# A new order of work in the prologue of a gated cross-attention and expert layer on one core

## The reference, cut to what matters

```python
x = x + tanh(g_xattn[0]) * xattn(layernorm(x), ctx, w_sim, b_sim, W_qv, b_qv)
x = x + tanh(g_ffn[0]) * ffn(layernorm(x), w_router, b_router, w1, b1, w2, b2)

def xattn(e, c, w_sim, b_sim, W_qv, b_qv):        # e: 4096 x 512, c: 3202 x 512
    w1, w2, w3 = w_sim[:d], w_sim[d:2*d], w_sim[2*d:]
    Sim = (e @ w1)[:, None] + (c @ w2)[None, :] + (e * w3) @ c.T + b_sim[0]
    hq_hat = softmax(Sim, axis=1) @ c
    hc_bar = softmax(max(Sim, axis=1)) @ e
    feats = concat([e, hq_hat, e * hq_hat, e * hc_bar])
    return feats @ W_qv + b_qv
```

## Time and the profile before

| | |
|---|---|
| time, median of 3 runs | 2228.9 us (2227.05 to 2230.01) |
| the profiled execution | 2228.91 us, span 2227.2 us |
| mean granted TensorE clock | 0.995 |
| PE busy | 2174.8 us |
| DVE busy | 1306.1 us |
| ACT busy | 1148.6 us |
| first block of scores on PE | from 30.93 us |
| first block of the steady loop on PE | from 71.66 us |

### The profile page before, as it was taken

One profiled execution on the slowest core, in us unless ns is written; L12 is line 12 of the kernel. 1 busy time (PEld: TensorE's weight loads), 2 busy tenths in 40 slices (PEclk: granted clock), 3 DMA queues, 4 the chain that ended last, 5 costly groups with the idle time before them and its releaser, 6 DMA issues.

```text
span 2227.2 us, 34525 instructions
## 1 busy us (share of the span) xinstructions
PE 2174.8 (98%) x12099; PEld 1129.0 (51%) x12099; DVE 1306.1 (59%) x2734; ACT 1148.6 (52%) x1747; POOL 144.8 (7%) x142
## 2 busy tenths in 40 slices
PE   5999999999999999999999997999999999999997
PEld 2444444444444444444454454656556565647464
DVE  7755566555556655554667785664656464646450
ACT  6755565565556556555533443535445363526260
POOL 0000000000000000000022222010101010010101
PEclk9999999999999999999999999999999999999999
DMA  9534444444444444344887863433333334343411
GB/s 250 132 80 106 107 113 99 112 98 91 106 108 110 98 115 98 84 103 112 246 238 207 210 174 91 145 102 104 99 107 95 108 94 112 91 118 119 128 41 24
DMA packets 485232, 266.06 MB, mean 119 GB/s; under 512 B 424388, under 2 KB 424772, under 8 KB 481084
## 3 DMA queue, kind: packets, MB, share of 16 engines
q1 hardware_dynamic: 474156, 244.90, 41.9%
q0 software_dynamic: 11024, 20.52, 4.7%
HBM read 97.96 MB, written 71.52 MB: 76 GB/s over the span
## 4 chain that ended last, share of the span: by engine, by line
PE 94%; DMA 2%; DVE 2%; SPq 1%; ACT 1%; issue 1%; POOL 0%; ACTq 0%; DVEq 0%; POOLq 0%
PE ps L1239 23%; PE ps L1255 22%; PE ps L2057 18%; PE ps L2072 18%; PE ps L1734 10%; DMA arena<-arena 1%; PE ps L369 1%; PE ps L1742 1%; DMA arena<-in_ctx 1%; PE ps L2084 0%; DVE arena L764 0%; PE ps L1755 0%; DMA arena<-in_L_ffn_w 0%; SPq L251 0%; PE ps L1251 0%
## 5 line engine op out<-in xcount | busy, mean ns | idle before, releaser
L1239 PE MATMUL ps<-arena 128*128 128x512 f16 (+1 forms) x2688 | 557.6, 358 | 4.4 <-DMA arena<-arena 2.7
L1255 PE MATMUL ps<-arena 128*128 128x512 f16 x2400 | 553.2, 379 | 0.4 <-DMA arena<-arena 0.4
L2057 PE MATMUL ps<-arena 128*128 128x320 f16 x3072 | 419.3, 299 | 3.3 <-DMA arena<-rows 3.1
L2072 PE MATMUL ps<-arena 128*128 128x512 f16 x1872 | 405.4, 379 | 0.0
L1239 PEld LDWEIGHTS ps<-arena 128*128 128x128 f16 x2688 | 250.3, 98 | 285.6 <-issue 5.7
L1255 PEld LDWEIGHTS ps<-arena 128*128 128x128 f16 x2400 | 233.5, 98 | 276.3 <-DMA arena<-arena 0.8
L1062 ACT ACTIVATE arena<-ps,arena 128x512 f32<-128x512 f32 (+1 forms) x224 | 163.5, 731 | 389.6 <-PE ps L1239 389.6
L2057 PEld LDWEIGHTS ps<-arena 128*128 128x128 f16 x3072 | 300.1, 98 | 122.7 <-DMA arena<-rows 4.7
L2072 PEld LDWEIGHTS ps<-arena 128*128 128x128 f16 x1872 | 183.1, 98 | 219.7
L780 DVE TENSOR_REDUCE arena<-arena 128x1 f32<-128x512 f32 (+1 forms) x224 | 139.8, 625 | 192.3 <-ACT arena L1062 191.6
L793 DVE SCALAR_TENSOR_TENSOR arena<-arena 128x512 f16<-128x512 f32 x192 | 144.1, 751 | 184.6 <-ACT arena L1083 184.6
(11 more groups left out here) (253 smaller groups left out, 1422.1 us busy)
## 6 DMA issues: line engine op xcount, KB each, us to landing
arena<-in_L_ffn_w SPq DMA_DIRECT2D x64, 1024.0 KB, 9.0
feats<-arena SPq DMA_DIRECT2D x48, 512.0 KB, 2.8
arena<-in_x SPq DMA_DIRECT2D x32, 512.0 KB, 3.4
rows<-arena SPq DMA_DIRECT2D x13, 774.0 KB, 3.8
out<-arena SPq DMA_DIRECT2D x16, 512.0 KB, 3.0
arena<-in_ctx SPq DMA_DIRECT2D x6, 1024.0 KB, 13.5
arena<-arena SPq DMA_TRANSPOSE x276, 3.1
arena<-in_L_xattn_W_qv SPq DMA_DIRECT2D x4, 1024.0 KB, 5.8
```

The source lines that it names most:

```text
L1239: mm = pe.matmul(out, qT[:, q, s * KD + k, :], ctxT[:, r * KD + k, a:z], start=(k == 0 and s + r == 0), stop=(k == KD - 1 and s == 1))
L1255: mm = pe.matmul(psO[q], turned, ctxN[:, j, r, :], start=(j + s + r == 0), stop=False)
L2057: mm = pe.matmul(psH[:, f % 2, h, :], w1s[:, s, k * F + f * P:k * F + (f + 1) * P], XT[:, r, k, h * HALF:(h + 1) * HALF], start=(k + s + r ...
L2072: mm = pe.matmul(psO[:, t % 2, :], hT[:, f, s, t * P:(t + 1) * P], w2s[:, r, f * D:(f + 1) * D], start=(f + s + r == 0), stop=(f == KF - 1 ...
```

## The change

The order of the prologue's work changes on all engines but GpSimd. SP issues the seven loads of the context one after the other, and the loads of the second pair of x, of `w1b` and of `bs` after them. Tiles 0 to 5 instead of 0 to 3 are turned on PE (`PET` = 6); of the two more, one is copied out by DVE and one by ACT. The two query units are turned into PSUM banks 3 and 2, ahead of the first scores. PE makes the first scores of both units in turn by chunk. ACT and DVE follow with their lists: among them `norm_hi(0)` and `norm_lo(0)` come early, `squares` comes earlier against `split_high`, `norm_weight(0)` and `tail_low` come before the last five maxima of unit 0, and ACT makes the first four probabilities of unit 0 before it moves out the blocks of unit 1's last three chunks.

```diff
@@ -400,7 +400,9 @@
     LAST = NC - 1
     XR = 4
     BLANKS = 3
-    FIRST = ((0, 1, 2, 3, 5, 7, 8), (4, 6, 9, 10, 11, 12, 13))
+    FIRST = ((1, 2, 4, 5, 8, 9, 10), (0, 3, 6, 7, 11, 12, 13))
+    MAXES0 = 9
+    PET = 6
     assert TILES[LAST][1] - TILES[LAST][0] == 2 and JT == 2 * NPAIR
 
     take, off = cutter(arena)
@@ -451,7 +453,7 @@
     psN = [ps[:, 4 + n, 0:NC] for n in range(2)]
     psV = ps[:, 7, 0:P]
     psT = [ps[:, 6 + n, :].bitcast(F16).rearrange("p (k i) -> p k i", i=P) for n in range(2)]
-    psQ = ps[:, 3, :].bitcast(F16).rearrange("p (k i) -> p k i", i=P)
+    psQ = [ps[:, 3 - n, :].bitcast(F16).rearrange("p (k i) -> p k i", i=P) for n in range(2)]
     psY_first = ps[:, 2:4, :]
     psX, psH = ps[:, 0, 0:P], ps[:, 1, 0:KD + 1]
 
@@ -621,16 +623,15 @@
             .then_inc(w23_loaded, 16)
         load_ctx(0)
         load_ctx(1)
-        sp.dma_start(w1b, w_sim[0:D].partition_broadcast(P)).then_inc(w1_loaded, 16)
-        sp.dma_start(bs, b_sim.partition_broadcast(P)).then_inc(w1_loaded, 16)
-        load_ctx(2)
-        load_x(1)
-        for c in range(3, NC):
+        for c in range(2, NC):
             load_ctx(c)
         sp.wait_ge(tail_zero, 1)
         for r in COPIES:
             sp.dma_start(raw[r:r + JR, JT - 1, :], ctx[(JT - 1) * P:J, :]).then_inc(tail_loaded, 16)
-        for j in range(TC, JT):
+        load_x(1)
+        sp.dma_start(w1b, w_sim[0:D].partition_broadcast(P)).then_inc(w1_loaded, 16)
+        sp.dma_start(bs, b_sim.partition_broadcast(P)).then_inc(w1_loaded, 16)
+        for j in range(PET, JT):
             turn_ctx(j)
         load_x(2)
         turn_q(2, 0)
@@ -933,71 +934,72 @@
                                  ALU.mult, ALU.add))
         s.link(dve.tensor_scalar(qrow, qscale, 1 / LN_SCALE, None, ALU.mult))
         query_rows(0, 0, 0, rowbuf[0], 0)
+        norm_lo(0)
         query_rows(0, 0, 1, rowbuf[1], 2)
+        query_lo(0, 0, rowbuf[0])
         chunk_scale(0)
+        query_lo(1, 1, rowbuf[1])
+        chunk_scale(1)
         dve.wait_ge(made, 6)
         dve.tensor_copy(ident, identf).then_inc(eye, 1)
-        chunk_scale(1)
         split_low(0)
         split_low(1)
-        split_low(2)
         chunk_scale(2)
         turned(0)
+        split_low(2)
+        turned(1)
+        turned(2)
         split_low(3)
-        query_lo(0, 0, rowbuf[0])
-        turned(1)
+        turned(3)
+        dve.wait_ge(q0_done, 2)
+        dve.tensor_copy(qT[:, 1], psQ[1]).then_inc(q0_ready, 1)
         split_low(4)
-        turned(2)
         chunk_scale(3)
+        norm_stats(1)
         split_low(5)
-        turned(3)
         split_low(6)
+        turned(4)
+        chunk_scale(4)
+        norm(1)
         split_low(7)
-        chunk_scale(4)
-        query_lo(1, 1, rowbuf[1])
+        query_rows(2, 1, 0, row0, 0)
         split_low(8)
+        chunk_scale(5)
         split_low(9)
-        chunk_scale(5)
+        split_low(10)
         chunk_max(FIRST[0][0], 0, 0)
-        dve.wait_ge(q0_done, 2)
-        dve.tensor_copy(qT[:, 1], psT[0]).then_inc(q0_ready, 1)
-        split_low(10)
         split_low(11)
+        chunk_scale(6)
+        common_scale()
+        split_low(12)
         chunk_max(FIRST[0][1], 0, 1)
-        chunk_scale(6)
-        norm_stats(1)
-        chunk_max(FIRST[0][2], 0, 2)
-        split_low(12)
-        norm(1)
-        query_rows(2, 1, 0, row0, 0)
-        common_scale()
-        chunk_max(FIRST[0][3], 0, 3)
         query_lo(2, 0, row0)
         chunk_max(FIRST[1][0], 1, 0)
-        norm_lo(0)
-        chunk_max(FIRST[0][4], 0, 4)
         chunk_max(FIRST[1][1], 1, 1)
-        chunk_max(FIRST[0][5], 0, 5)
-        chunk_max(FIRST[0][6], 0, 6)
-        row_max(0, 0, UNIT0)
         dve.wait_ge(w1_loaded, 32)
         norm_weight(0)
         tail_low()
+        chunk_max(FIRST[0][2], 0, 2)
+        chunk_max(FIRST[0][3], 0, 3)
+        chunk_max(FIRST[0][4], 0, 4)
+        chunk_max(FIRST[0][5], 0, 5)
+        chunk_max(FIRST[0][6], 0, 6)
+        row_max(0, 0, MAXES0)
         low(0, 0, 0)
         chunk_max(FIRST[1][2], 1, 2)
         low(0, 0, 1)
+        low(0, 0, 2)
         chunk_max(FIRST[1][3], 1, 3)
-        low(0, 0, 2)
         chunk_max(FIRST[1][4], 1, 4)
         low(0, 0, 3)
         query_rows(3, 1, 1, row0, 0)
         chunk_max(FIRST[1][5], 1, 5)
         low(0, 0, 4)
-        chunk_max(FIRST[1][6], 1, 6)
-        row_max(1, 1, 2 * NC)
         low(0, 0, 5)
         query_lo(3, 1, row0)
+        chunk_max(FIRST[1][6], 1, 6)
         low(0, 0, 6)
+        row_max(1, 1, 2 * NC)
         pool_top(0, 0, 0)
         value_scale()
         pool_rows(0, 0, 0)
@@ -1035,6 +1037,10 @@
                 act.wait_ge(c_lo, p - 1)
             act.activation(ctxN[:, 2 * p:2 * p + 2, 0, :], raw[:, 2 * p:2 * p + 2, :], ACT.Identity,
                            bias=zero[:, 0:1], scale=gscale[:, 2 * p // TC:2 * p // TC + 1]).then_inc(c_hi, 1)
+
+        def turned(j):
+            act.wait_ge(ct_done, j + 1)
+            act.copy(ctxT[:, :, j * P:(j + 1) * P], psT[j % 2]).then_inc(ct_out[j % 2], 1)
 
         def query_high(u, q, row, ready):
             act.wait_ge(row_step, ready)
@@ -1132,56 +1138,57 @@
         act.wait_ge(made, 4)
         act.activation(warm, zero, ACT.Sqrt, bias=lneps[:, 0:1], scale=1.0)
         norm_sd(0)
+        norm_hi(0)
         squares(0)
         query_high(0, 0, rowbuf[0], 2)
         squares(1)
+        query_high(1, 1, rowbuf[1], 4)
+        squares(2)
         split_high(0)
-        squares(2)
         split_high(1)
+        act.wait_ge(q0_done, 1)
+        act.copy(qT[:, 0], psQ[0]).then_inc(q0_ready, 1)
         split_high(2)
         split_high(3)
         squares(3)
         split_high(4)
+        squares(4)
         split_high(5)
-        squares(4)
-        act.wait_ge(q0_done, 1)
-        act.copy(qT[:, 0], psQ).then_inc(q0_ready, 1)
         split_high(6)
+        squares(5)
+        turned(5)
+        norm_sd(1)
         split_high(7)
-        squares(5)
-        query_high(1, 1, rowbuf[1], 4)
-        scores(FIRST[0][0], 0, 0, 0)
         split_high(8)
+        squares(6)
+        scores(FIRST[1][0], 0, 1, 0)
+        scores(FIRST[0][0], 1, 0, 0)
         split_high(9)
-        squares(6)
-        scores(FIRST[0][1], 1, 0, 1)
         split_high(10)
+        query_high(2, 0, row0, RK * 2 + 2)
         split_high(11)
-        scores(FIRST[0][2], 2, 0, 2)
-        norm_sd(1)
-        scores(FIRST[0][3], 3, 0, 3)
+        scores(FIRST[0][1], 2, 0, 1)
+        scores(FIRST[1][1], 3, 1, 1)
+        scores(FIRST[0][2], 0, 0, 2)
+        scores(FIRST[0][3], 1, 0, 3)
         split_high(12)
-        scores(FIRST[1][0], 0, 1, 0)
-        query_high(2, 0, row0, RK * 2 + 2)
-        scores(FIRST[0][4], 1, 0, 4)
-        scores(FIRST[1][1], 2, 1, 1)
-        norm_hi(0)
-        scores(FIRST[0][5], 3, 0, 5)
-        scores(FIRST[0][6], 0, 0, 6)
-        scores(FIRST[1][2], 1, 1, 2)
+        scores(FIRST[1][2], 2, 1, 2)
+        scores(FIRST[1][3], 3, 1, 3)
+        scores(FIRST[0][4], 0, 0, 4)
+        scores(FIRST[0][5], 1, 0, 5)
+        scores(FIRST[0][6], 2, 0, 6)
         act.wait_ge(common, 4)
         probabilities(0, 0, 0)
         probabilities(0, 0, 1)
-        scores(FIRST[1][3], 2, 1, 3)
+        probabilities(0, 0, 2)
+        probabilities(0, 0, 3)
         scores(FIRST[1][4], 3, 1, 4)
-        probabilities(0, 0, 2)
+        probabilities(0, 0, 4)
         scores(FIRST[1][5], 0, 1, 5)
-        scores(FIRST[1][6], 1, 1, 6)
-        probabilities(0, 0, 3)
-        probabilities(0, 0, 4)
         probabilities(0, 0, 5)
         query_high(3, 1, row0, RK * 3 + 2)
         probabilities(0, 0, 6)
+        scores(FIRST[1][6], 1, 1, 6)
         pool_weight(0)
         half(1, 0, first=True)
         half(1, 1, first=True)
@@ -1225,8 +1232,11 @@
         def first_scores(q, c):
 
             n = FIRST[q][c]
-            if c:
-                pe.wait_ge(ct_turned[c], 16 * (TILES[c][1] - TILES[c][0]))
+            a, z = TILES[c]
+            for v in range(2):
+                pe.wait_ge(ct_out[v], min(z, PET) // 2)
+            if z > PET:
+                pe.wait_ge(ct_turned[c], 16 * (z - max(a, PET)))
             if n >= 4:
                 pe.wait_ge(scores_ready, n - 3)
             scores(n % 4, q, c)
@@ -1279,36 +1289,35 @@
         pe.wait_ge(made, 3)
         sums(0)
         sums(1)
+        pe.wait_ge(eye, 1)
+        turn_query(0, psQ[0])
         sums(2)
-        pe.wait_ge(eye, 1)
         turn(0)
         turn(1)
+        turn(2)
+        turn_query(1, psQ[1])
+        turn(3)
         sums(3)
-        turn(2)
-        turn_query(0, psQ)
-        turn(3)
-        sums(4)
-        pe.wait_ge(q0_ready, 1)
-        for v in range(2):
-            pe.wait_ge(ct_out[v], 2)
-        first_scores(0, 0)
-        first_scores(0, 1)
-        sums(5)
-        first_scores(0, 2)
-        turn_query(1, psT[0])
-        sums(6)
-        first_scores(0, 3)
+        turn(4)
+        turn(5)
```

(13 more changed lines are left out.)

## The result

The changed kernel takes 2234.59 us (median; 2233.23 to 2236.21) against 2228.54 for the one before, measured beside it: ratio 1.0025, 95% interval 1.0016 to 1.0034. One of its twelve executions was a slow one of 8390.89 us, which the range and the ratio leave out; without it the median is 2234.37. The ratio makes the change 5.6 us slower, the two medians differ by 6.05. The time is inside the range on record (2226 to 2235) but 4.1 above the number (2230.5), and on the side that had a chance of 0.18. The profiled execution took 2233.70, with a span of 2232.0, 4.8 more than before.

What follows compares the result with a forecast made beforehand. PE bounds the kernel, and the steady loop's start, hung on unit 0's softmax, decides. Start 0.4 us earlier, low clock 1.9 us dearer: +1.5 on 2228.9 gives 2230.4, as a number 2230.5 us; range 2226 to 2235.

Steps and rivals of the forecast that it cites:

- the side that had a chance of 0.18: Whole kernel: the outcome slower, by over about 0.2% (4.5 us).
- Tiles and queue: SP's transposes: tile 6 enters at 25.5, 20 transposes instead of 22, tile 25 lands at 56.0, before at 57.9.
- PE: Prologue scores: start about 27.3, unit 0's last block ends 57.0, first 14 blocks done about 62.9, 8 us earlier.
- DVE at `tail_low`: Before unit 0's last five maxima: DVE stands from about 52.6 to 56.05 for tile 25; row maximum at 59.25.
- upper bound of 58.8: Tile 25's landing if the first transpose is slow (2.81 against 1.37) and the split chain starts one load later.
- The table load: ACT before unit 0's first exponential: load lies ahead of the wait, so covered; uncovered it would cost 0.4 us.
- The hop: ACT's list before the loop: PE's start needs the fifth high part, two hops of 4.75 us; loop at 71.2.
- The clock: Loop's start after 8 us of PE standing: low clock costs 1.9 us, bounds 0 and 2.1.
- Passes to the end one for one: From the loop's first block on: a shift of its start reaches the end whole; later waits in the loop cost nothing.
- (A): SP's transposes: tiles come late and `tail_low` hands it on, slower by over 0.2%, about 2234.5 us; chance 0.18.
- (B): Loop's start: it starts when PE is done, 62.9, warm, 8.8 us earlier, 2220 us; chance 0.08.
- (D): PE's prologue scores: tiles or scales hold a block, unit 0's last block ends behind 58; chance 0.07, within the band.

Runs made afterwards that it cites:

- Filling PE: The changed kernel with 40 matmuls of 128x512, result unread, between PE's last first score and the steady loop: 2232.00 us, ratio 1.0013.
- four tiles: The changed kernel with tiles 4 and 5 turned by DMA again, so only four on TensorE: 2235.39 us, ratio 1.0027.
- thirteen kernels of the table: The changed kernel and the follow-up kernels built on it or on the kernel before; median shifts against the kernel before from -4.93 to +6.62 us.
- four more edits: The changed kernel with ACT's block order put back, `tail_low` behind the row maximum, exponential table loaded ahead, 15th block moved out earlier: 2223.98 us, ratio 0.9975.
- one kernel (65.80, 2.75): The changed kernel with ACT moving blocks (1,4) and (1,5) after unit 0's second probability, (1,6) after the third: 2227.55 us, ratio 0.9993.
- three edits: The changed kernel with ACT's block order put back, `tail_low` behind the row maximum and the exponential's table loaded ahead: 2225.63 us, ratio 0.9987.

## Why the prediction was right, and where it was off

**Tiles and queue: right.** Tile 25 was put at 56.0 and was there at 56.3; 20 transposes from 26.13 to 53.00, first expected at 25.5.

**PE: right at the end, wrong on the way.** Unit 0's last block was put at 57.0, all 14 at 62.9; PE was done at 63.28. I had 1.9 us for the low clock at the first scores; they ran at the full pace from the start (2.76), and PE lost about as much in three waits (0.71, 1.18, 0.27) that the walk did not have.

**DVE at `tail_low`: right.** Row maximum 59.25 expected, 59.71 measured. (The upper bound of 58.8 for tile 25 does not follow: 56.0 with the two terms named beside it, 1.44 and 1.15, is 58.6.)

**The table load: wrong.** The step "the table load lies ahead of the wait, so it is covered" failed. I took it from one row, the load at 92.40 ahead of a square root. At the first exponential the load came behind the row maximum, though ACT had stood free for 1.87 us: 1.28 us, confirmed by moving it. In the kernel's text the square root has one wait and the first exponential two; whether that makes the difference, no run tests. The price on record for the other case, "uncovered it would cost 0.4", was wrong as well: it cost 1.28 in the trace and 1.21 of the start. This is two thirds of the 1.95 by which the loop started late; most of the rest is the row maximum (0.46).

**The hop: right,** the step that mattered. 4.75 twice expected, 4.84 and 4.75 measured, and shown two ways: both hops taken out (start 7.35 earlier), and one hop put alone into the kernel before (4.4 later). Filling PE left the start where it was, so PE's stand is a consequence and not a cause.

**The clock: right in kind,** 1.9 taken, 1.55 measured by filling the pause. The bound of 2.1 on record held here but is no general one: with four tiles the block took 5.13, 2.4 over 2.75. The Trainium skill's account (TensorE: Matmul & The Clock Gate, What's actually happening), the low rate after idleness and activity to release it, agrees with both signs here: 4.30 after 9.9 us of standing, 2.75 when filled.

**"Passes to the end one for one": off.** In the loop it does. Behind the landmark the account does not close: the medians lie 0.5 to 3.0 us above the landmark's shift in all thirteen kernels of the table, 1.8 for the changed one in its profile and 3.0 by median. The kernels with no shift to pass on lie 0.6 and 0.7 above it, so about that much may belong to the one profile of the kernel before, which all are compared with. The wait near 1086 is scatter as far as the profiles tell; the one near 1123 (0.96 here) is there in all nine kernels built on the changed one, its cause unknown. The rest is open. I had put the later stages at nothing without a reason, and they are the largest part of the error: from 2230.4, +1.95 for the late start, -0.35 for the clock, +3.0 behind the landmark and -0.4 because the kernel before took 2228.54 here and not 2228.9 make 2234.6.

**Luck.** That the time lay within the range is in part luck. The upper end of 2235 was there to take in rival (A), which did not occur; the load and the later stages, neither of which was in the sum, brought the time to the same place.

**Rivals.** (A), late tiles, gave nearly the measured time for a reason that did not occur. (B) is what the change could have brought: with four more edits it gives 4.9 of its 8.8. (D) occurred in small, inside PE's slack.

## What to carry to other kernels

When a reordered prologue brings one engine home earlier, follow the next consumer's wait to the instruction that releases it and count what now stands ahead of that instruction on its engine: here two more probabilities in ACT's list, each tied to a transpose by a two-tile staging buffer, turned 8 us of earlier scores into a later start. After each such release look for the next wait in line before claiming the gain: three stood behind each other (13th, 15th, 16th block). A queue that gets fewer items but a later first item may end at the same time.

## What the runs showed of the hardware

- With six tiles turned on PE just ahead, the last of them after a stand of 0.84 us, the first block of scores took 2.76 us, the full pace; with four tiles and 1.57 us of standing ahead of it, 4.22. Of the two differences, the transposes and the standing, no run separates one from the other.
- A pause of 2.50 us left the granted clock at 1.00 in one kernel (65.80, 2.75), and one of 2.02 in the same kernel was followed by a low one (78.34, 4.45; 0.66 in its first 1.7 us). With three edits a pause of 2.06 left it at 1.00 (77.39, 2.76).
- A table load of ScalarE (1.28 us) can stand before or behind the wait of the instruction that needs it: before it at 92.40 in the kernel before, behind it at 59.80 in the changed one.
